# First-layer attention products four heads side by side, row sums from a tile of ones and from GpSimd, and the low parts of the second layer's queries and keys subtracted by GpSimd

## Chip, core and metric

The kernel runs on one core of one Trainium2 chip. The metric is the device time of one execution in microseconds; three executions of the kernel before gave 1474.76, 1475.09 and 1475.23 us, median 1475.09 us. The core's engines are TensorE (PE, with its weight loads shown apart as PEld), VectorE (DVE), ScalarE (ACT), GpSimd (POOL) and SyncE (SP, which here only issues DMAs).

## The reference

Two transformer layers over a sequence of 2048 tokens of width 128, all in float32. Each line of the sketch ends in a layer norm over the residual sum.

```python
x = layernorm(x + attention0(x))   # 8 heads in 2 groups, keys and values from 32 latents per group, causal softmax
x = layernorm(x + ffn0(x))         # 128 -> 352 -> 128, silu(gate) * up, inputs and weights rounded to blockwise FP4
x = layernorm(x + attention1(x))   # 16 heads of 8 in 4 groups, biases, softmax over all 2048 keys
x = layernorm(x + experts(x))      # 8 experts 128x128, softmax gate with a threshold of 0.1
```

In both attentions `scores = q k^T * scale`, `probs = softmax(scores)`, `y = probs v`. The kernel keeps `exp(scores - max)` and divides by its row sum (the denominator) at the end.

## The kernel before

**Tiling.** Queries are worked in chunks `c` of QC = 512 (NC = 4 chunks), keys in tiles `kt` of P = 128 (16 tiles). Heads come in groups `g` of HG = 4. One *iteration* is one `(layer, c, g)`. The first layer has 8 iterations and is causal: chunk `c` sees `4 (c + 1)` key tiles, of which the last four are *diagonal* (narrower: 512, 384, 256, 128 queries, and their triangle is zeroed by `clip` on POOL). The second layer has 16 iterations of 16 key tiles.

**One unit** is a key tile of one head. It is a score product on PE (L726 in the first layer, `KO0` by `QO`; L730 in the second, `KO1` by `Q1`; float32r) into a score bank of PSUM, an exponential on ACT (L926) into one of the 8 slots of `PR`, and a product with the values on PE (L749). The first layer has 2 score banks, the second 3. The product with the values is full float32, so each is two matmul instructions in a trace. A score product of unit `u` waits for the exponential of unit `u - 2` (first layer). An exponential waits until the product of the unit 8 earlier has read its slot.

**Values and denominators.** `V0[:, tile, g, :]` is VW0 = 64 wide: 32 latents and then ones, so that column 32 of the result is the denominator. Two heads stand side by side on the columns of PE (64 each), and two banks (`OUT_BANKS` 4 and 5) hold the four heads. In the second layer the values are VW1 = 32 wide (8 values, then ones), and four heads stand side by side in one bank.

**Order.** One list of steps is made at build time and each engine walks through it in order. `iteration` yields the four scores of a tile, with *side steps* spread between them, and behind every `SIDE_BY_SIDE[layer]` scores (2 in the first layer, 4 in the second) the products of as many heads of the tile before. Side steps use 4 further PSUM banks in turn (`side_full`, `side_free`). Most of them are `max`: the next iteration's scores laid out queries by keys (PE L655 in the first layer, L650 in the second), whose row maxima DVE takes (L1161, on the diagonal L1158). The others are the projections (`q0`, `k0`, `v0`, `q1`, `k1`, `v1`), the output of the iteration before (`out_copy` by ACT into `OS`, transposes L661, `out0` or `out1` on DVE), and the rest of the layer for the chunk before (`attended0`: output projection, norm, quantisation of x, gate and up; `rest0`: quantisation of h, down, norm, `k1`, `v1`; `chunk1`: the second layer's norm, gate and experts).

**High and low parts.** A float32 query or key is kept as a float32r number and a remainder. For `k0` and `q0` only rows of the result are subtracted. For `q1` and `k1` (32 and 16 of them, 128x512 each) ACT writes rows into `Q1` or `KO1` with a mask as the scale (L840, L848), and DVE then writes bank plus bias minus that into the same tile (L1102, `tails`) and frees the side bank.

**POOL** has `clip` (L996, 128 in the first layer), `rstd` (L988, 16) and the sums over experts (L1003, L1005).

## Time and profile before

| | |
|---|---|
| median of the three timed runs | 1475.09 us |
| the profiled execution's own time | 1470.66 us |
| its span, first to last instruction | 1468.9 us |
| PE busy | 1311.4 us, 89% |
| DVE busy | 1088.7 us, 74% |
| ACT busy | 845.8 us, 58% |
| POOL busy | 110.8 us, 8% |
| mean granted TensorE clock | 0.929 of full speed |

The page divides the span among engines, follows back the chain of work that ended last, and groups instructions by line and shape. The idle time shown beside an instruction is that of its engine just before it, with what released it. A matmul's own duration contains its pipeline; how often matmuls follow each other is read from their starts.

### The profile page before, as it was taken

The numbers are of one execution on the slowest core, as the hardware profiler recorded it, in microseconds if no ns is written. First come the engines' busy times: TensorE is split into PE (matmuls) and PEld (weight loads), VectorE is DVE, ScalarE is ACT, GpSimd is POOL, SyncE is SP. The second block draws the span as 40 slices with busy tenths as digits, with TensorE's granted clock in tenths as the row PEclk, the third lists the DMA queues.
The fourth block names the chain that finished last, engine by engine and source line by source line (L and its number), as shares of the span: only waits on it lengthen the run. The fifth ranks groups of instructions, "written<-read, shape, count | busy, mean of one in ns | idle before, by whom it ended". The sixth has DMA issues, their size and how long they took to land.

```text
span 1468.9 us, 19049 instructions
## 1 busy us (share of the span) xinstructions
PE 1311.4 (89%) x6337; PEld 563.3 (38%) x6337; DVE 1088.7 (74%) x2289; ACT 845.8 (58%) x1621; POOL 110.8 (8%) x227
## 2 busy tenths in 40 slices
PE   4688889889999965899999999999999999999884
PEld 3354445344443432433333333333433333333322
DVE  3677696688645668778888788888879888987324
ACT  2445535554555421177777666777666776777660
POOL 2010010001010100000000002000110000000033
PEclk9669899899999975689999999999999999999897
DMA  3000000000000000000000000000000000000000
GB/s 100 1 1 1 1 1 1 0 1 1 1 1 1 0 1 0 1 1 1 2 1 1 1 1 9 1 1 1 1 1 8 1 1 2 1 1 1 1 8 8
DMA packets 9010, 6.13 MB, mean 4 GB/s; under 512 B 2184, under 2 KB 8272, under 8 KB 8912
## 3 DMA queue, kind: packets, MB, share of 16 engines
q1 hardware_dynamic: 8912, 4.91, 1.2%
q8 instruction: 51, 0.84, 0.2%
q14 instruction: 47, 0.39, 0.1%
HBM read 3.66 MB, written 1.05 MB: 3 GB/s over the span
## 4 chain that ended last, share of the span: by engine, by line
PE 71%; DVE 15%; ACT 7%; issue 4%; POOL 1%; DMA 1%; SPq 1%; DVEq 0%; POOLq 0%; ACTq 0%
PE ps L749 24%; PE ps L730 16%; PE ps L650 8%; DVE MP L1161 7%; PE ps L726 6%; ACT PR L926 4%; PE ps L655 4%; PE ps L646 2%; PE ps L712 2%; ACT QO L825 1%; PE ps L661 1%; PE ps L679 1%; DVE ps L1158 1%; PE ps L615 1%; PE ps L690 1%
## 5 line engine op out<-in xcount | busy, mean ns | idle before, releaser
L926 ACT ACTIVATE PR<-ps 128x512 f32<-128x512 f32 (+2 forms) x1344 | 699.1, 585 | 414.1 <-PE ps L730 224.3
L1161 DVE TENSOR_REDUCE MP<-ps 128x1 f32<-128x512 f32 x1216 | 764.2, 682 | 133.9 <-PE ps L650 87.4
L749 PE MATMUL ps<-PR,V 128*32 128x512 f32 (+2 forms) x2688 | 435.6, 605 | 0.7 <-ACT OS L825 0.7
L730 PE MATMUL ps<-Q,KO 64*128 64x512 f32 x1024 | 363.1, 466 | 26.6 <-ACT PR L926 20.6
L650 PE MATMUL ps<-KO,Q 64*128 64x512 f32 x1024 | 354.5, 447 | 16.3 <-DVE MP L1161 12.2
L730 PEld LDWEIGHTS ps<-Q,KO 64*128 64x128 f32 x1024 | 153.6, 186 | 350.3 <-ACT PR L926 290.3
L650 PEld LDWEIGHTS ps<-KO,Q 64*128 64x128 f32 x1024 | 164.4, 191 | 85.0 <-DVE MP L1161 47.9
L726 PE MATMUL ps<-QO,KO 97*128 97x512 f32 (+3 forms) x320 | 144.7, 464 | 21.2 <-ACT PR L926 18.8
L655 PE MATMUL ps<-KO,QO 96*128 96x512 f32 (+2 forms) x320 | 127.9, 441 | 19.5 <-DVE QO L1137 13.7
L749 PEld LDWEIGHTS ps<-PR,V 128*32 128x32 f32 (+1 forms) x2688 | 74.1, 116 | 130.6 <-issue 60.4
L726 PEld LDWEIGHTS ps<-QO,KO 97*128 97x128 f32 x320 | 62.8, 201 | 152.0 <-ACT PR L926 97.0
L655 PEld LDWEIGHTS ps<-KO,QO 96*128 96x128 f32 x320 | 66.7, 214 | 43.2 <-DVE QO L1137 15.3
L1158 DVE CUSTOM_DVE_ANT_0 ps<-ps,mask_qk 128x128 f32<-128x128 f32 (+3 forms) x128 | 62.8, 493 | 20.8 <-PE ps L655 20.4
L996 POOL TENSOR_SCALAR_AFFINE_SELECT PR<-PR 128x128 f32<-128x128 f32 x128 | 39.0, 307 | 396.2 <-ACT PR L926 395.3
L988 POOL TENSOR_TENSOR RS<-VE,const 128x4 f32<-128x4 f32 x16 | 16.2, 1010 | 660.0 <-DVE VE L1091 660.0
L1102 DVE SCALAR_TENSOR_TENSOR Q<-ps,bq,Q 128x512 fp32r<-128x512 f32 x32 | 24.0, 750 | 39.9 <-ACT Q L840 30.2
L1137 DVE TENSOR_TENSOR QO<-ps,QO 32x512 fp32r<-32x512 f32 x32 | 22.0, 688 | 25.7 <-ACT QO L825 25.4
L1003 POOL TENSOR_TENSOR qa<-qa 128x512 f32<-128x512 f32 (+2 forms) x24 | 19.7, 821 | 225.3 <-DVE XQ L1206 216.2
L712 PE MATMUL ps<-ew,XQT 128*128 128x512 f32 x64 | 36.2, 665 | 0.0
L646 PE MATMUL ps<-XT,WQ 128*128 128x512 f32 x64 | 35.6, 638 | 0.0
L825 ACT ACTIVATE HQT<-ps 128x256 f32<-128x256 f32 (+2 forms) x36 | 11.0, 354 | 37.4 <-PE ps L685 33.8
L840 ACT ACTIVATE Q<-ps,bq_low,const 128x512 fp32r<-128x512 f32 x32 | 24.9, 777 | 7.7 <-PE ps L646 7.7
(179 smaller groups left out, 748.7 us busy)
## 6 DMA issues: line engine op xcount, KB each, us to landing
Q<-MR SPq DMA_DIRECT2D x64, 2.0 KB
result<-V SPq DMA_DIRECT2D x4, 256.0 KB, 2.3
H<-in_L_attn_wq SPq DMA_DIRECT2D x1, 512.0 KB, 6.7
HQT<-in_L_attn_wo SPq DMA_DIRECT2D x1, 512.0 KB, 5.0
ew<-in_L_ffn_expert_w SPq DMA_DIRECT2D x1, 512.0 KB
bq<-in_L_attn_bq SPq DMA_DIRECT2D x12, 0.1 KB
wd<-in_L_ffn_w_down SPq DMA_DIRECT2D x1, 176.0 KB, 3.7
wg<-in_L_ffn_w_gate SPq DMA_DIRECT2D x1, 128.0 KB, 4.4
```

Of the source, the lines that this page charges most:

```text
L646: last = nc.tensor.matmul(bank[:, :], WQ13[:, g, pair, :, :], XT[:, c * QC:(c + 1) * QC], start=True, stop=True)
L650: last = nc.tensor.matmul(bank[:, :], Q1[rows, buf, h // 2, q * P:(q + 1) * P], KO1[rows, g, kc * QC:(kc + 1) * QC], start=True, stop=True)
L655: last = nc.tensor.matmul(bank[:, 0:n], QO[0:SHIFT, buf, h, q * P:(q + 1) * P], KO0[0:SHIFT, g, kc * QC:kc * QC + n], start=True, stop=True)
L712: last = nc.tensor.matmul(bank[:, :], X2T[:, q * P:(q + 1) * P], ew[:, 4 * e:4 * e + 4, :], start=True, stop=True)
L726: m = nc.tensor.matmul(dst[:, q0:QC], KO0[:, g, kt * P:(kt + 1) * P], QO[:, buffer_of(0, it), h, q0:QC], start=True, stop=True)
L730: m = nc.tensor.matmul(dst[:, :], KO1[rows, g, kt * P:(kt + 1) * P], Q1[rows, it, h // 2, :], start=True, stop=True)
L749: nc.tensor.matmul(dst, VO[layer][:, kt, g, :], PR[:, u % NP_RING, q0:QC], start=kt == 0, stop=kt == key_tiles(layer, c) - 1).then_inc(pv_ ...
L825: return nc.scalar.activation(out, in_, ACT.Copy)
L926: nc.scalar.activation(PR[:, u % NP_RING, q0:QC], ps[:, 8 - nb + u % nb, q0:QC], ACT.Exp, scale=SCALE[layer]).then_inc(exp_done, 1)
L996: nc.gpsimd.affine_select(block, block, [[1, P]], ALU.is_ge, nothing, base=0, channel_multiplier=-1).then_inc(clipped, 1)
L1158: v.tensor_tensor_reduce(bank[:, 0:w], bank[:, 0:w], mask_qk[:, QC - w:QC], 1.0, LOWEST, ALU.add, ALU.max, MP[:, buf, h, q, kc:kc + 1]).th ...
L1161: v.tensor_reduce(MP[:, buf, h, q, kc:kc + 1], bank[:, 0:w], AX, ALU.max).then_inc(free, 1)
```

## The change

1. In the first layer the values are 32 wide (`VW0` 64 to 32, no ones in `V0`), four heads stand side by side, and their products go into one bank (5) once per tile. `SIDE_BY_SIDE` becomes (4, 4).
2. The first layer's denominators come from products of a tile of ones (`ones`, 128x32) with the same `PR` slots, four heads side by side into bank 4 (`denominators`).
3. For some tiles (`by_pool`: below the diagonal, tile 0 and the odd ones) there is no such product. POOL adds the `PR` slots of these tiles up (`add_up`, into `ADDED[h]`: two halves of `ew` and two of a new tile `more`), and at the iteration's end one product of ones with each sum adds them in. Chunks 1, 2 and 3 have 3, 5 and 7 such tiles in each of their two iterations, and 8, 16 and 24 additions of 128x512. An exponential waits as well until POOL has read its slot (`added`).
4. For `q1` and `k1` ACT writes two tiles from the bank (`WHOLE`, a ring of two, with the bias; then `Q1` or `KO1` as before) and frees the bank; POOL subtracts one from the other. PE's `max` waits for POOL (`tailed`) in place of DVE.
5. `out0` becomes one reciprocal over the bank of denominators and one multiplication over that of products, in place of two of each.
6. The experts' weights are loaded when the second layer's products begin, since `ew` serves as `ADDED` before. Some weights move into other tiles' space.

```diff
-VW0, VW1 = 64, 32
+VW0, VW1 = 32, 32
+        WHOLE = (sb("WHOLE", [P, QC])[:, :], flat(wgu[:, 0:QC // D, :]))
+        more = sb("more", [P, NE, D])
+        ADDED = [x[:, j * QT:(j + 1) * QT, :].rearrange("p e d -> p (e d)") for x in (ew, more) for j in range(2)]
+        def by_pool(layer, c, kt):
+            return layer == 0 and kt < c * QT and (kt == 0 or kt % 2 == 1)
...
+            def denominators(c, kt, n, u, q0):
+                last = kt == key_tiles(0, c) - 1
+                if not by_pool(0, c, kt):
+                    if diagonal(0, c, kt):
+                        pe.wait_ge(clipped, n.clips + clips_at[0] + HG - 1)
+                    else:
+                        pe.wait_ge(exp_done, n.units + u + 4 + HG)
+                    for h in range(HG):
+                        nc.tensor.matmul(ps[h * VW0:(h + 1) * VW0, OUT_BANKS[0], q0:QC], ones[:, :], PR[:, (u + h) % NP_RING, q0:QC],
+                                         start=kt == (2 if c else 0), stop=last and c == 0)
+                if last and c > 0:
+                    added_at[0] += added_in(c)
+                    pe.wait_ge(added, n.added + added_at[0])
+                    for h in range(HG):
+                        nc.tensor.matmul(ps[h * VW0:(h + 1) * VW0, OUT_BANKS[0], :], ones[:, :], ADDED[h],
+                                         start=False, stop=True)
...
-                if layer == 0:
-                    dst = ps[(h % 2) * VW0:(h % 2 + 1) * VW0, OUT_BANKS[h // 2], q0:QC]
-                else:
-                    dst = ps[h * VW1:(h + 1) * VW1, OUT_BANKS[0], q0:QC]
+                if layer == 0 and h == 0:
+                    denominators(c, kt, n, u, q0)
+                dst = ps[h * VW1:(h + 1) * VW1, OUT_BANKS[1 - layer], q0:QC]
...
+                if kind in BY_POOL:
+                    t = tails_at[0]
+                    if t >= len(WHOLE):
+                        act.wait_ge(tailed, t + 1 - len(WHOLE))
+                    dst, bias, low_bias, low = of_parts(item)
+                    nc.scalar.activation(WHOLE[t % len(WHOLE)], bank, ACT.Identity, bias=bias)
+                    i = nc.scalar.activation(dst, bank, ACT.Identity, bias=low_bias, scale=low)
+                    tails_at[0] += 1
...
                         act.wait_ge(pv_done, n.units + u + 1)
+                        if u >= NP_RING and add_of[u - NP_RING]:
+                            act.wait_ge(added, add_of[u - NP_RING])
...
+            def add_up(h, unit, sums, first):
+                p = PR[:, unit % NP_RING, :]
+                pool.wait_ge(exp_done, unit + 5)
+                if first:
+                    nc.gpsimd.tensor_tensor(ADDED[h], PR[:, (unit - HG) % NP_RING, :], p, ALU.add).then_inc(added, 1)
+                else:
+                    pool.wait_ge(added, sums + 1 - HG)
+                    nc.gpsimd.tensor_tensor(ADDED[h], ADDED[h], p, ALU.add).then_inc(added, 1)
...
+                        if by_pool(layer, c, kt):
+                            if kt == 1 and h == 0:
+                                pool.wait_ge(pv_done, NP_RING + n.units + units - HG)
+                            if kt > 0:
+                                add_up(h, n.units + units, n.added + sums, kt == 1)
+                                sums += 1
...
+                    if kind in BY_POOL:
+                        pool.wait_ge(side_free[k % NS], n.side // NS + k // NS + 2)
+                        dst = of_parts(step)[0]
+                        nc.gpsimd.tensor_tensor(dst, WHOLE[tails % len(WHOLE)], dst.bitcast(f32),
+                                                ALU.subtract).then_inc(tailed, 1)
...
-            def tails(dst, bank, bias):
-                return v.scalar_tensor_tensor(dst, bank, bias, dst.bitcast(f32), ALU.add, ALU.subtract)
...
                 if kind == "out0":
-                    b = item[1]
-                    o = bank.rearrange("p (q h l) -> p q h l", q=QT, h=2)
-                    rec = OR[:, :, 0:2]
-                    link(v.reciprocal(rec, o[:, :, :, LAT]))
-                    v.tensor_tensor(ON[:, :, :].rearrange("p q (h l) -> p q h l", l=LAT)[:, :, 2 * b:2 * b + 2, :],
-                                    o[:, :, :, 0:LAT], rec.unsqueeze(3).broadcast_to([P, QT, 2, LAT]), ALU.mult).then_inc(free, 1)
+                    o = bank.rearrange("p (q h l) -> p q h l", q=QT, h=HG)
+                    if item[1] == 0:
+                        v.reciprocal(OR[:, :, :], o[:, :, :, 0]).then_inc(free, 1)
+                        return
+                    v.tensor_tensor(ON[:, :, :].rearrange("p q (h l) -> p q h l", l=LAT), o,
+                                    OR[:, :, :].unsqueeze(3).broadcast_to([P, QT, HG, LAT]), ALU.mult).then_inc(free, 1)
```

PE in the last iteration of the first layer (c = 3, g = 1), before: one key tile, two heads at a time behind every second score (L726 is a score, L650 a `max` of the second layer, L749 a product).

```order
L749 MATMUL ps<-PR,V 64x512 x2
L726 MATMUL ps<-QO,KO 128x512
L650 MATMUL ps<-KO,Q 128x512
L726 MATMUL ps<-QO,KO 128x512
L749 MATMUL ps<-PR,V 64x512 x2
```

The same place after the change (L762 is the score, L686 the `max`, L721 transposes of H, L778 the product with ones, L802 the product with the values): two key tiles, the first with products alone behind it, the second with denominators too.

```order
L802 MATMUL ps<-PR,V 32x512 x4
L762 MATMUL ps<-QO,KO 128x512
L686 MATMUL ps<-KO,Q 128x512
L762 MATMUL ps<-QO,KO 128x512 x2
L686 MATMUL ps<-KO,Q 128x512
L762 MATMUL ps<-QO,KO 128x512
L721 MATMUL ps<-const,H 128x128 x2
L721 MATMUL ps<-const,H 96x128
L778 MATMUL ps<-PR,ones 32x512 x4
L802 MATMUL ps<-PR,V 32x512 x4
```

Between two bursts of products there are now four scores, where there were two; a `max` stands behind two of the four.

POOL from c = 2, g = 0 to the start of c = 3, g = 0, before (L996 is `clip`, L988 is `rstd`):

```order
L996 AFFINE_SELECT PR<-PR 128x128 x24
L988 TENSOR_TENSOR RS<-VE,const 128x4
L996 AFFINE_SELECT PR<-PR 128x128 x8
L988 TENSOR_TENSOR RS<-VE,const 128x4
```

After the change, from the end of c = 2, g = 1 into the first seven key tiles of c = 3, g = 0 (L1081 is `clip`, L1063 `rstd`, L1118 the subtraction for `k1`, L1070 and L1073 the additions):

```order
L1081 AFFINE_SELECT PR<-PR 128x128
L1118 TENSOR_TENSOR KO<-wgu,KO 128x512
L1070 TENSOR_TENSOR ew<-PR 128x512 x2
L1070 TENSOR_TENSOR more<-PR 128x512 x2
L1073 TENSOR_TENSOR ew<-ew,PR 128x512
L1063 TENSOR_TENSOR RS<-VE,const 128x4
L1073 TENSOR_TENSOR ew<-ew,PR 128x512
L1073 TENSOR_TENSOR more<-more,PR 128x512 x2
```

POOL's queue, which held short clips and the `rstd`, now has four additions for every second key tile, and the `rstd` stands among them.

## Rows read from the trace of the kernel before

**Rows 1.** The page's fourth part: the chain that ended last, by engine.

```profile
PE 71%; DVE 15%; ACT 7%; issue 4%; POOL 1%; DMA 1%; SPq 1%; DVEq 0%; POOLq 0%; ACTq 0%
```

**Rows 2.** Busy time by stage: start:end, length, engines' busy us (count), PE clock.

```profile
118.00:173.00 55.00, 46.31 (x198) 23.85 (x197) 40.52 (x106) 33.84 (x60) 5.91 (x17) 0.95 0.00 1
173.00:233.00 60.00, 52.39 (x220) 27.92 (x220) 49.07 (x134) 23.21 (x51) 6.06 (x17) 0.90 0.00 1
233.00:307.00 74.00, 66.20 (x264) 31.34 (x262) 49.60 (x123) 42.85 (x75) 5.87 (x17) 0.93 0.00 1
307.00:374.00 67.00, 64.38 (x278) 32.05 (x277) 58.90 (x151) 32.01 (x67) 6.33 (x17) 0.97 0.00 1
374.00:448.00 74.00, 70.14 (x284) 30.97 (x284) 38.91 (x96) 41.28 (x78) 5.66 (x17) 0.98 0.00 1
448.00:523.00 75.00, 73.97 (x287) 29.69 (x287) 44.02 (x98) 38.57 (x77) 5.63 (x17) 1.00 0.00 1
523.00:626.00 103.00, 67.45 (x179) 33.74 (x181) 77.23 (x175) 15.30 (x27) 2.01 (x2) 0.63 0.00 0
626.00:1371.00 745.00, 719.69 (x4030) 278.75 (x4030) 633.06 (x1106) 533.40 (x1025) 28.44 (x37) 0.99 0.01 2
```

**Rows 3.** Instructions grouped by line and shape: count, busy us, mean ns, idle before.

```profile
L749 PE MATMUL ps<-PR,V 128*32 128x512 f32 x2048 | 276.7, 613 | 0.0
L749 PE MATMUL ps<-PR,V 128*64 128x512 f32 x448 | 126.5, 644 | 0.7 <-ACT OS L825 0.7
...
L840 ACT ACTIVATE Q<-ps,bq_low,const 128x512 fp32r<-128x512 f32 x32 | 24.9, 777 | 7.7 <-PE ps L646 7.7
L1102 DVE SCALAR_TENSOR_TENSOR Q<-ps,bq,Q 128x512 fp32r<-128x512 f32 x32 | 24.0, 750 | 39.9 <-ACT Q L840 30.2 <-PE ps L650 8.9 <-PE ps L664 0.8
...
L825 ACT ACTIVATE OS<-ps 128x512 f32<-128x512 f32 x32 | 18.4, 608 | 7.3 <-PE ps L749 7.2
...
L1003 POOL TENSOR_TENSOR qa<-qa 128x512 f32<-128x512 f32 x8 | 10.2, 1273 | 224.1 <-DVE XQ L1206 216.2 <-DVE qa L1212 7.8
```

**Rows 4.** Timeline in c = 3, g = 0: start us, duration us, instruction.

```profile
405.23 0.72 PE L726 MATMUL ps<-QO,KO 97*128 97x512 f32 x2
...
405.79 0.39 PE L655 MATMUL ps<-KO,QO 96*128 96x512 f32 x1
...
406.11 1.08 PE L749 MATMUL ps<-PR,V 128*64 128x512 f32 x4
...
407.12 0.73 PE L726 MATMUL ps<-QO,KO 97*128 97x512 f32 x2
```

**Rows 5.** Timeline in c = 3, g = 1.

```profile
465.18 0.50 PE L726 MATMUL ps<-QO,KO 97*128 97x512 f32 x1
...
465.61 0.50 PE L650 MATMUL ps<-KO,Q 64*128 64x512 f32 x1
465.72 0.60 ACT L926 ACTIVATE PR<-ps 128x512 f32<-128x512 f32 x1 [0.84 <-PE ps L726]
...
466.04 0.50 PE L726 MATMUL ps<-QO,KO 97*128 97x512 f32 x1
...
466.47 1.08 PE L749 MATMUL ps<-PR,V 128*64 128x512 f32 x4
```

**Rows 6.** Timeline in the second layer, products four side by side.

```profile
689.39 1.07 PE L749 MATMUL ps<-PR,V 128*32 128x512 f32 x8
...
690.39 0.50 PE L730 MATMUL ps<-Q,KO 64*128 64x512 f32 x2
...
690.92 2.06 ACT L926 ACTIVATE PR<-ps 128x512 f32<-128x512 f32 x4 [0.76 <-PE ps L730]
...
691.57 0.18 PEld L730 LDWEIGHTS ps<-Q,KO 64*128 64x128 f32 x1 [0.43 <-ACT PR L926]
```

**Rows 7.** All clips on POOL: durations in ns (minimum/median/maximum), first and last start.

```profile
L996 POOL TENSOR_SCALAR_AFFINE_SELECT PR<-PR x128: 292/292/673, 53.1 to 521.0; 128x128 f32<-128x128 f32 x128
```

**Rows 8.** Timeline of POOL and DVE where a clip met a quantising step.

```profile
205.37 0.49 POOL L996 TENSOR_SCALAR_AFFINE_SELECT PR<-PR 128x128 f32<-128x128 f32 x1 [4.61 <-ACT PR L926]
...
205.38 0.34 DVE L1069 TENSOR_SCALAR qc<-qc 128x352 f32<-128x352 f32 x1
```

More of the change, by code:

```diff
@@ L475, in __init__ @@
                 self.heads = sum(k in IN_PARTS for k in kinds)
+                self.tails = sum(k in BY_POOL for k in kinds)
                 self.rstd = sum(k in ("y0", "down", "y1", "stats") for k in kinds)
@@ L478, in __init__ @@
                 self.logits = kinds.count("logits")
+                self.added = sum(s[0] == "scores" and s[5] > 0 and by_pool(s[1], s[2], s[5]) for s in steps)
                 self.clips = sum(s[0] == "scores" and diagonal(s[1], s[2], s[5]) for s in steps)
@@ L507, in build @@
         program = padded(program)
+        UNITS0 = sum(s[:2] == ("scores", 0) for s in program)
         def parts(engine, walk):
@@ L551, in walk @@
             def walk(steps, n, lag):
-                k, chunks = 0, 0
+                k, chunks, units, experts = 0, 0, 0, False
                 for step in steps:
+                    units += step[0] == "scores"
+                    if step[0] == "products" and step[1] == 1 and not experts:
+                        experts = True
+                        sp.wait_ge(pv_done, NP_RING + UNITS0)
+                        sp.dma_start(ew[:, :, :], A["L1_ffn_expert_w"].rearrange("e k n -> k e n")).then_inc(ld["experts"], 16)
                     if step[0] == "shift":
@@ L808, in walk @@
                         pe.wait_ge(ld["attn1"], N_ATTN1)
-                        pe.wait_ge(ld["moe"], 64)
+                        pe.wait_ge(ld["moe"], 48)
+                    if step == ("expert", 0, 0):
+                        pe.wait_ge(ld["experts"], 16)
                     if kind == "wgT":
@@ L1008, in walk @@
             def walk(steps, n, lag):
-                k, rs, tiles, units = 0, 0, 0, 0
+                k, rs, tiles, tails, units, sums = 0, 0, 0, 0, 0, 0
                 for step in steps:
@@ L1012, in walk @@
                     if kind == "scores":
-                        if diagonal(*step[1:3], step[5]):
-                            clip(n.units + units, first_query(*step[1:3], step[5]))
+                        _, layer, c, g, it, kt, h = step
+                        if diagonal(layer, c, kt):
+                            clip(n.units + units, first_query(layer, c, kt))
+                        if by_pool(layer, c, kt):
+                            if kt == 1 and h == 0:
[3 more added lines that the diff above has]
+                                sums += 1
                         units += 1
```

81 lines of the change are left out of this document (47 added, 34 removed).

## The prediction

> **What bounds the kernel now.** I read the chain that ended last first: 71% of it is PE and 15% DVE [rows 1], so PE time is what counts, if it is saved where PE is the one that is late. That is read by stage [rows 2]. The six rows from 118 to 523 us are the iterations c = 1 to 3 of the first layer, two per chunk. In c = 3 PE is busy 70.1 of 74 us and 74.0 of 75, and DVE only 38.9 and 44.0: whatever PE saves there comes off the time. In the g = 1 iterations of c = 1 and c = 2 DVE is busy 49.1 of 60 us and 58.9 of 67, because they carry the quantisation of h and more maxima than scores. There a PE that is faster soon meets DVE. From 523 to 626 us, the end of the first layer, DVE leads (77 of 103 us, PE clock 0.63). From 626 to 1371 us, the second layer, PE is busy 720 of 745 us, DVE 633 and ACT 533. The change alters no PE work there.
>
> **Products of the first layer.** A pair of 64-wide products over 512 queries starts at 406.11 and the next score at 407.12 us: 1.01 us [rows 4]. Four 32-wide ones start at 689.39, the next score at 690.39: 1.00 us [rows 6]. The busy times agree: 126.5 us over 448/4 = 112 pairs is 1.13, 276.7 over 2048/8 = 256 fours is 1.08 [rows 3], each with some 0.1 us of the last one's pipeline in it. So a tile costs 2.02 us now, and will cost 1.00 if POOL sums it and 2.00 if the tile of ones does. The chunks 1 to 3 have 2 x (3 + 5 + 7) = 30 summed tiles. That is 30 x 1.02 = 30.6 us less PE time, against 6 x 1.00 = 6 us for the last products with the sums. The 26 other tiles of 512 queries and the narrow ones cost what they did. This 24.6 us is the gross term; the rest is about what becomes of it.
>
> **Bursts.** Two bursts per tile become one, with four scores between. That has two effects. From the first of two scores to the burst, with one maximum, takes 406.11 - 405.23 = 0.88 us for three matmuls, so the steps beside a burst are some 0.1 us longer than those within; one burst fewer saves about 0.1 to 0.2 us a tile. Against it, with two score banks the third score must wait for the first one's exponential, which used to run under the pair between. The score starts at 465.18, its exponential at 465.72 (0.54 later) and takes 0.60 [rows 5]; another waiting score starts (691.57) 0.05 after the exponential that it needs ends (690.92 + 0.60). So the third score starts no earlier than 0.54 + 0.60 + 0.05 = 1.19 us after the first. The fourth waits for an exponential that ends 0.52 later (four take 2.06 [rows 6]), so 1.71, and the burst starts 0.32 after it (405.79 to 406.11 [rows 4]): 2.03 us.
>
> - c = 3, g = 0: a tile has four scores and mostly two maxima. Now it takes 2 x 1.89 = 3.78 us [rows 4]. Afterwards 2.03 + 1.00 = 3.03 (summed, -0.75) or 4.03 (+0.25). With 7 summed, 6 others and the last product: -5.3 + 1.5 + 1.0 = -2.8 us.
> - c = 3, g = 1: matmuls of different row counts follow each other in 0.43 us (465.18, 465.61, 466.04), so half a tile takes 1.29 + 1.01 = 2.30 us and a tile 4.60. Afterwards, as the order shows, a maximum stands behind two of the four scores: 1.19 + 3 x 0.43 = 2.48, and 3.48 (-1.12) or 4.48 (-0.12). -7.8 - 0.7 + 1.0 = -7.5 us.
> - c = 2 and c = 1, g = 0: about one maximum or more behind each score, so that PE reaches the third score at 1.0 us or later anyway and the exponential is covered. I take -1.12 and -0.12: -5.6 - 0.5 + 1.0 = -5.1 us, and -3.4 - 0.2 + 1.0 = -2.6 us.
> - c = 2 and c = 1, g = 1: the same on PE, but DVE has 8.1 and 10.9 us of idle time [rows 2] in many short pieces, and gives back 4 x 0.75 = 3 us in each for the keys' subtractions. I take 2 us and 1 us.
>
> The sum is -2.8 - 7.5 - 5.1 - 2.6 - 2 - 1 = -21.0 us. The chunk c = 0 has no summed tile and is counted as nothing: its PE time is the same, and the waits for the clips of all four heads lie one tile behind.
>
> **The additions on POOL.** The nearest row is the experts' sum, 128x512 with two inputs in SBUF: 1.27 us [rows 3]. Four of them take 5.1 us per two tiles, and two tiles will take 3.03 + 4.03 = 7.1 us, so POOL keeps up in the steady part. At an iteration's start it does not quite: tile 0's slots are freed only by the additions of tile 1, so the exponential of head 3 of tile 2 waits for the fourth addition. That ends 4 x 1.27 = 5.1 us after tile 1's first exponential, where ACT would like the slot about 4 us after it. The output steps of the iteration before stretch these tiles; I take 0.4 us each in six iterations, +2.4 us (bounds 0 and 1.1 each, 6.6 in all). The clips and `rstd` queue behind additions. The first diagonal tile's clips come some 5 us after the last additions begin, and its products a tile later: nothing. `rstd` also holds up the additions behind it until DVE's statistics are there; a slot is wanted back two tiles (7 us) later, which covers it.
>
> **POOL against DVE.** A clip takes 292 ns at the median but 0.49 us where it met a VectorE step from SBUF to SBUF (205.37 us) [rows 7, 8]. The additions are four times longer, and DVE's quantising steps may stand behind them: in c = 1 and 2, g = 1 DVE is the one that can least afford it. The values of 1 and 2 us above already hold some of this. The Trainium skill, in "SBUF — State Buffer", section "Who interferes with whom", says more: a DVE step with two SBUF inputs or in a 2-port mode and a GpSimd step share a port pair, and whoever comes second is blocked for the whole of the other. By the clip's row the trace agrees as far as it goes; by the rule, 16 additions of 1.27 us in 67 us would meet a third of some 24 such steps and hold each for about 0.6 us, 5 us of DVE in c = 2, g = 1, and that iteration would then gain nothing.
>
> **The low parts.** Per tile DVE loses 0.75 us, ACT gains a copy between the 0.61 us of an output copy and the 0.78 of the masked one, POOL gains 1.27 [rows 3]. For 24 to 28 queries in the second layer: ACT has 745 - 533 = 212 us of idle time there and takes 28 x 0.65 = 18 more. PE's third score bank and the burst of products (1.00 us) cover most of it. DVE, 85% busy, loses 21 us. Both can hold PE; I take -1 us, bounds -8 (half of DVE's relief reaches PE) and +9 (half of ACT's copies do). The queries are asked for half an iteration ahead, so POOL's latency is hidden. At the first layer's end it is not: the last keys are needed at once, and ACT's copy and POOL's 1.27 in place of DVE's 0.75 make them 0.6 + 1.27 - 0.75 = 1.1 us later, of which DVE's own relief gives back half: +0.5 us. `out0` costs DVE what it did within 0.3 us and is off the path. The experts' load moves to 626 us, some 200 us before its first use, and waits for products long done.
>
> **Sum.** -21.0 + 2.4 - 1 + 0.5 = -19.1 us. Against the profiled execution's own 1470.66 us (span 1468.9, 1.8 around it) that is 1451.6. The runs' median, 1475.09, is 4.4 higher, and I forecast for such runs: 1475.1 - 19.1 = 1456 us.
>
> **Rivals.**
> - *The gross term arrives.* The exponentials' wait is hidden by the maxima and DVE does not limit: 24.6 us, and one burst fewer in some 80 tiles at 0.1 to 0.15, so -33 us, 1442 us. For it: PE above 95% in c = 2, g = 1 and c = 3. Against: 1.19 us is longer than the 0.9 us that PE needs for two scores and two maxima.
> - *Only c = 3 gains.* DVE, slowed by the additions, or the PE clock (0.90 to 0.95 in c = 1 and the start of c = 2) eats the rest: -10 us with the start's waits, 1466 us. For it: DVE at 82 and 88% in rows 2, and the clip's 0.49 us.
> - *POOL becomes the bound (slower).* Place: the `PR` slots of odd tiles. Two tiles take 7.1 us, so it decides once four additions take longer, at 1.77 us each; there are 24 such pairs. At 2.0 us it costs 24 x 0.9 = 22 us and the change is about even; at 2.2 us 24 x 1.7 = 41, and 1475 - 19 + 41 = 1497 us. For it: the clip's maximum of 673 ns is over twice its median. Against: 1.27 us in every row of the experts' sums.
> - *Nothing in net*: the second layer's +9 and the bound of the start's waits, 1475 - 21 + 6.6 + 9 + 1 = 1471 us or more.
>
> **Chances and range.** Forecast (1448 to 1461) 0.45, the gross term (1438 to 1448) 0.17, only c = 3 (1461 to 1470) 0.23, nothing in net (1470 to 1478) 0.07, POOL the bound 0.08. The range 1441 to 1470 leaves out the last two and a little of the second. A measurement here can tell about 0.2%, 3 us. Faster than that: 0.45 + 0.17 + 0.23 + 0.02 = 0.87; within it 0.05; slower 0.08.
>
> **What would show it.** The groups of the changed profile: 32-wide products 1.00 us apart in the first layer, additions at 1.27 us. Stages: c = 3, g = 1 some 7 us shorter and g = 0 only some 3, with PE idle before scores on ACT there; c = 1 and c = 2, g = 1 nearly as long as before; the second layer within 2 us of 745. Wrong if ACT waits for POOL's additions beyond each iteration's third tile, if the additions take 1.8 us or more, or if DVE's quantising steps are much longer than they are (0.34 us in rows 8).

## The result: 1.06% slower, and the profile after

The changed kernel takes 1490.89 us (median of 4 runs, 1490.33 to 1490.99) against 1475.16 for the kernel before, a ratio of 1.0106 with a 95% interval of 1.0089 to 1.0124. The forecast was 1456 us, faster. The profiled execution took 1490.83 us. Now and then an execution runs at a low clock throughout (e2's profiled one took 1605.3 us at 0.72); medians and ratios here leave these out. The page's first and fourth part of the changed kernel:

```profile
PE 1299.7 (87%) x6785; PEld 564.5 (38%) x6785; DVE 1090.1 (73%) x2225; ACT 870.2 (58%) x1669; POOL 294.6 (20%) x371
...
PE 67%; DVE 17%; ACT 8%; issue 4%; POOL 2%; DMA 1%; SPq 1%; DVEq 0%; POOLq 0%; ACTq 0%
```

PE is busy 11.7 us less than before, and the kernel is 20 us longer in these two profiles (the kernel before's profiled execution is 4.5 us under its median). PE's share of the last chain fell from 71% to 67% [rows 1] and DVE's rose from 15% to 17%.

**Where.** I cut both traces at the copies of the results to `OS`, which end each iteration. Windows of the changed kernel (start:end, length, busy us of PE, PEld, DVE, ACT, POOL with counts, PE clock): c = 0, g = 1; then c = 1, 2, 3 with g = 0 and 1 each; then all seven.

```profile
89.70:120.00 30.30, 27.17 (x142) 16.38 (x142) 22.43 (x66) 11.53 (x38) 3.93 (x13) 0.76 0.00 1
120.00:176.30 56.30, 45.13 (x247) 23.87 (x247) 41.55 (x102) 33.51 (x59) 16.15 (x25) 0.91 0.00 1
176.30:240.50 64.20, 50.70 (x266) 28.71 (x266) 50.97 (x127) 25.83 (x55) 22.25 (x29) 0.87 0.00 1
240.50:315.10 74.60, 63.24 (x329) 31.66 (x328) 55.59 (x120) 42.53 (x74) 26.76 (x33) 0.91 0.00 1
315.10:393.10 78.00, 68.26 (x340) 34.88 (x341) 60.35 (x143) 34.19 (x70) 31.49 (x37) 0.85 0.00 1
393.10:463.70 70.60, 63.90 (x367) 30.12 (x367) 46.04 (x98) 42.87 (x81) 38.39 (x43) 0.98 0.00 1
463.70:537.60 73.90, 69.87 (x368) 29.40 (x367) 49.33 (x87) 40.17 (x82) 42.13 (x46) 0.98 0.00 1
89.70:537.60 447.90, 388.28 (x2054) 195.01 (x2053) 326.26 (x741) 230.62 (x453) 181.10 (x225) 0.90 0.00 1
```

The same cut of the kernel before, all seven (c = 2, g = 1 stands in [rows 2], within 0.1 us).

```profile
89.30:522.50 433.20, 399.58 (x1638) 191.76 (x1637) 303.52 (x767) 223.71 (x438) 39.26 (x116) 0.95 0.00 1
```

The lengths, c = 0, g = 1 to c = 3, g = 1: before 28.0, 54.6, 60.3, 73.9, 66.9, 74.7, 74.8; after 30.3, 56.3, 64.2, 74.6, 78.0, 70.6, 73.9. So the first layer lost 14.7 us, 11.1 of them in c = 2, g = 1. PE is busy 11.3 us less in it and idle 26.0 more (447.9 - 388.3 = 59.6, against 33.6), and its clock is 0.90 in place of 0.95. At two levels, 1.2 and 2.4 GHz, a mean of 0.90 means that the lower one held for about 447.9 x 0.10 x 2 = 90 us; before it was about 433.2 x 0.05 x 2 = 43 us. In c = 2, g = 1 alone PE is idle 9.7 us (78.0 - 68.3), before 2.7, and busy 4 us longer on 4 us less work. From the first layer's last copy to the start of the second layer's last iteration it is 856.6 us, before 856.7; the last iteration takes 55.9 in place of 49.9. It has the same instructions; 20 us around its start ran at 0.51 of the clock where those of before had 0.74 (first row after, second row before):

```profile
1391.00:1411.00 20.00, 19.34 (x69) 7.36 (x73) 2.58 (x13) 11.11 (x23) 0.00 (x0) 0.51 0.00 0
```

```profile
1374.00:1394.00 20.00, 18.19 (x80) 6.73 (x80) 2.58 (x13) 12.46 (x25) 0.00 (x0) 0.74 0.01 1
```

**How.** The timeline of the changed kernel in c = 2, g = 1 (start us, us, instruction, in brackets the engine's idle time before it and what ended it):

```profile
327.26 0.51 DVE L1172 TENSOR_TENSOR qa<-qa,qc 128x352 f32<-128x352 f32 x1
...
327.88 2.78 POOL L1073 TENSOR_TENSOR ew<-ew,PR 128x512 f32<-128x512 f32 x2 [4.85 <-ACT PR L1001]
...
328.31 1.23 DVE L1174 TENSOR_TENSOR qa<-qa,qc 128x352 f32<-128x352 f32 x1
...
329.57 1.47 DVE L1176 TENSOR_TENSOR H<-qa,qs 128x352 f32<-128x352 f32 x1
330.62 2.78 POOL L1073 TENSOR_TENSOR more<-more,PR 128x512 f32<-128x512 f32 x2
...
331.72 0.55 PE L721 MATMUL ps<-const,H 128*128 128x128 f32 x3 [2.88 <-DVEq L1181]
...
332.26 1.12 PE L778 MATMUL ps<-PR,ones 128*32 128x512 f32 x8
...
333.14 1.95 PE L802 MATMUL ps<-PR,V 128*32 128x512 f32 x8
```

The same kind of step takes 0.51 us before POOL's additions begin, and 1.23 and 1.47 us under them. PE needs the quantised `H` for a transposition that stands in its queue ahead of the rest, and waits 2.88 us. Behind it the four products take 1.95 us where they took 1.07 [rows 6]: the granted clock is 1.00 from 326 to 333 us and 0.57 from 333 to 337. Wait and lower clock come together here. What waited, and for what (changed kernel, first layer; engine, line, released by: us in total, times, longest):

```profile
PE ps L762 <- ACT PR L1001: 24.9, 22, 4.1
PE ps L721 <- DVEq L1181: 12.7, 6, 4.0
PE ps L691 <- DVE MP L1252: 4.8, 9, 0.9
```

and of the kernel before:

```profile
PE ps L726 <- ACT PR L926: 18.8, 7, 3.7
PE ps L685 <- DVEq L1081: 3.5, 4, 1.6
...
PE ps L655 <- DVE MP L1161: 0.9, 3, 0.5
```

H's transpositions wait 9 us more, the scores 6 (e4 has these without any sum), the maxima 4. PE never waits for an addition, and ACT does so once, for 0.2 us. Groups of DVE steps by shape, changed kernel (count | busy, mean ns), and behind them those of the kernel before:

```profile
L1176 DVE TENSOR_TENSOR H<-qa,qs 128x352 f32<-128x352 f32 x12 | 9.3, 775 | 0.1
L1174 DVE TENSOR_TENSOR qa<-qa,qc 128x352 f32<-128x352 f32 x13 | 8.9, 684 | 0.2
...
L1169 DVE TENSOR_SCALAR qc<-qc 128x352 f32<-128x352 f32 x13 | 7.6, 586 | 0.2
```

```profile
L1074 DVE TENSOR_TENSOR qa<-qa,qc 128x352 f32<-128x352 f32 x13 | 6.8, 519 | 0.2
...
L1076 DVE TENSOR_TENSOR H<-qa,qs 128x352 f32<-128x352 f32 x12 | 6.2, 518 | 0.1
L1069 DVE TENSOR_SCALAR qc<-qc 128x352 f32<-128x352 f32 x13 | 4.4, 337 | 0.2
```

### The profile page after: what moved, and what is told of

It reads as the page before. It is cut to its first block, busy times and chain, and to the rows that moved or that the text cites. A ratio compares the mean times of both kernels' runs of the same rounds, so it can differ in the third digit from the quotient of the medians.

```text
span 1489.1 us, 20173 instructions
## 1 busy us (share of the span) xinstructions
PE 1299.7 (87%) x6785; PEld 564.5 (38%) x6785; DVE 1090.1 (73%) x2225; ACT 870.2 (58%) x1669; POOL 294.6 (20%) x371
## 3 DMA queue, kind: packets, MB, share of 16 engines
HBM read 3.66 MB, written 1.05 MB: 3 GB/s over the span
## 4 chain that ended last, share of the span: by engine, by line
PE 67%; DVE 17%; ACT 8%; issue 4%; POOL 2%; DMA 1%; SPq 1%; DVEq 0%; POOLq 0%; ACTq 0%
PE ps L802 20%; PE ps L766 16%; PE ps L686 7%; DVE MP L1252 7%; ACT PR L1001 5%; PE ps L762 4%; PE ps L691 3%; PE ps L778 2%; PE ps L748 2%; PE ps L682 2%; DVE ps L1249 1%; PE ps L697 1%; ACT QO L889 1%; PE ps L715 1%; PE ps L726 1%
## 5 line engine op out<-in xcount | busy, mean ns | idle before, releaser
L766 PE MATMUL ps<-Q,KO 64*128 64x512 f32 x1024 | 367.2, 471 | 27.2 <-ACT PR L1001 21.0
L686 PE MATMUL ps<-KO,Q 64*128 64x512 f32 x1024 | 351.5, 445 | 18.3 <-DVE MP L1252 13.5
L802 PE MATMUL ps<-PR,V 128*32 128x512 f32 (+1 forms) x2688 | 365.1, 616 | 0.0
L686 PEld LDWEIGHTS ps<-KO,Q 64*128 64x128 f32 x1024 | 163.5, 191 | 77.8 <-DVE MP L1252 40.6
L762 PE MATMUL ps<-QO,KO 97*128 97x512 f32 (+3 forms) x320 | 147.1, 469 | 27.5 <-ACT PR L1001 24.9
L691 PE MATMUL ps<-KO,QO 96*128 96x512 f32 (+2 forms) x320 | 131.3, 449 | 27.4 <-DVE QO L1233 14.7
L762 PEld LDWEIGHTS ps<-QO,KO 97*128 97x128 f32 x320 | 64.3, 203 | 129.0 <-ACT PR L1001 68.0
L1118 POOL TENSOR_TENSOR Q<-WHOLE,Q 128x512 fp32r<-128x512 f32 x16 | 20.5, 1280 | 452.0 <-ACT Q L923 452.0
L802 PEld LDWEIGHTS ps<-PR,V 128*32 128x32 f32 x2688 | 60.2, 111 | 120.6 <-issue 65.9
L1081 POOL TENSOR_SCALAR_AFFINE_SELECT PR<-PR 128x128 f32<-128x128 f32 x128 | 38.9, 309 | 181.9 <-ACT PR L1001 181.0
L1073 POOL TENSOR_TENSOR ew<-ew,PR 128x512 f32<-128x512 f32 x36 | 47.2, 1331 | 73.0 <-ACT PR L1001 73.0
L778 PE MATMUL ps<-PR,ones 128*32 128x512 f32 (+3 forms) x400 | 49.6, 571 | 1.2 <-POOL PR L1081 1.2
L1073 POOL TENSOR_TENSOR more<-more,PR 128x512 f32<-128x512 f32 x36 | 48.0, 1351 | 0.3 <-ACT PR L1001 0.3
L1118 POOL TENSOR_TENSOR Q<-wgu,Q 128x512 fp32r<-128x512 f32 x16 | 20.6, 1290 | 133.3 <-ACT Q L923 133.3
L1063 POOL TENSOR_TENSOR RS<-VE,const 128x4 f32<-128x4 f32 x16 | 16.2, 1015 | 121.8 <-DVE VE L1191 121.8
```

The lines of the kernel that those rows point to most:

```text
L686: last = nc.tensor.matmul(bank[:, :], Q1[rows, buf, h // 2, q * P:(q + 1) * P], KO1[rows, g, kc * QC:(kc + 1) * QC], start=True, stop=True)
L691: last = nc.tensor.matmul(bank[:, 0:n], QO[0:SHIFT, buf, h, q * P:(q + 1) * P], KO0[0:SHIFT, g, kc * QC:kc * QC + n], start=True, stop=True)
L762: m = nc.tensor.matmul(dst[:, q0:QC], KO0[:, g, kt * P:(kt + 1) * P], QO[:, buffer_of(0, it), h, q0:QC], start=True, stop=True)
L766: m = nc.tensor.matmul(dst[:, :], KO1[rows, g, kt * P:(kt + 1) * P], Q1[rows, it, h // 2, :], start=True, stop=True)
L778: nc.tensor.matmul(ps[h * VW0:(h + 1) * VW0, OUT_BANKS[0], q0:QC], ones[:, :], PR[:, (u + h) % NP_RING, q0:QC], start=kt == (2 if c else 0 ...
L802: nc.tensor.matmul(dst, VO[layer][:, kt, g, :], PR[:, u % NP_RING, q0:QC], start=kt == 0, stop=kt == key_tiles(layer, c) - 1).then_inc(pv_ ...
```

## The experiments

Each was timed with the kernel before on the same chip; ratios to it are what I compare (0.1% is 1.5 us; the runs lie on several chips). "The split kernel" is e6.

| kernel | bursts a tile | sums on POOL | low parts | median us | ratio (95%) |
|---|---|---|---|---|---|
| after | 1 | c = 1, 2, 3 | POOL | 1490.9 | 1.0106 (1.0089 to 1.0124) |
| e2 | 1 | c = 1, 2, 3 | DVE | 1488.1 | 1.0098 (1.0074 to 1.0122) |
| e1 | 1 | none | POOL | 1484.2 | 1.0074 (1.0046 to 1.0102) |
| e4 | 1 | none | DVE | 1481.6 | 1.0050 (1.0035 to 1.0065) |
| e3 | 1 | fills for additions | DVE | 1466.5 | 0.9962 (0.9942 to 0.9981) |
| e5 | 1 | c = 3 | DVE | 1467.8 | 0.9969 (0.9952 to 0.9986) |
| e9 | 2 | c = 1, 2, 3 | DVE | 1478.4 | 1.0026 (1.0009 to 1.0044) |
| e6 | 2 | none | DVE | 1467.4 | 0.9969 (0.9950 to 0.9988) |
| e8 | 2 | c = 3; c = 2, g = 0 | DVE | 1465.8 | 0.9954 (0.9934 to 0.9974) |
| e7 | 2 | c = 3 | DVE | 1460.9 | 0.9925 (0.9898 to 0.9951) |
| e16 | as e7 | | | 1461.6 | 0.9921 (0.9901 to 0.9942) |
| e10 | 2 | c = 3 | POOL | 1468.2 | 0.9956 (0.9937 to 0.9974) |
| e11 | 2 | c = 3, 8 of 12 tiles | DVE | 1469.3 | 0.9974 (0.9955 to 0.9993) |
| e12 | 2 | 48 idle, c = 1, 2 | DVE | 1483.5 | 1.0064 (1.0044 to 1.0084) |
| e13 | 2 | none, e12's start | DVE | 1468.2 | 0.9960 (0.9941 to 0.9979) |
| e14 | 2 | 48 idle fills, c = 1, 2 | DVE | 1479.7 | 1.0040 (1.0019 to 1.0062) |
| e15 | 2 | 48 idle, c = 3 | DVE | 1467.6 | 0.9960 (0.9939 to 0.9980) |

### e1, e2, e4: the parts of the change, one by one

e1 takes no sums (first pair of lines, in `by_pool`); e2 gives the low parts back to DVE, whose step is again as before; e4 does both.

```diff
-            return layer == 0 and kt < c * QT and (kt == 0 or kt % 2 == 1)
+            return layer == 0 and False and kt < c * QT and (kt == 0 or kt % 2 == 1)
...
-        IN_PARTS = ("q0", "k0")
-        BY_POOL = ("q1", "k1")
+        IN_PARTS = ("q0", "k0", "k1", "q1")
+        BY_POOL = ()
```

> No tile is summed on POOL: the product of ones is made for all 16 tiles, and the six last products with the sums fall away. POOL keeps the low parts. Theory A (POOL's additions hold up VectorE's quantising steps, PE then waits for H and its clock falls): c = 2, g = 1 comes back from 78 us to 68 to 72, c = 1, g = 1 from 64 to about 61, while c = 3 gets 4 to 5 us longer per iteration; in all 1476 to 1486 us. Rival B (the single burst per tile and the waits for exponentials cost the time): the time rises by the 24 us of PE products, to 1505 or more. Rival C (the low parts on ACT and POOL cost it): also above 1490.

> The changed kernel with the low parts of queries and keys as before the change (one copy by ACT, the subtraction by VectorE); the sums stay on POOL. Theory A: little changes, 1486 to 1493 us, c = 2, g = 1 still above 75 us. Rival C (the low parts cost it): 1475 to 1480 us.

> Both undone: products of ones for all tiles, low parts by VectorE; what is left of the change is four heads side by side, one burst per tile and the denominators in their own bank. PE does the same amount of products as the kernel before. Theory A: 1472 to 1480 us. Rival B (the burst): 1485 to 1492 us, with PE idle before scores on the exponentials.

Without any sum the kernel is still slower than before by 0.5 to 0.7%, though PE's work is the same. That points at the one long burst, which e6 tests; e4 lies above the theory's range and below the rival's. e2's ratio differs from that of the change by 0.0008, e1's from e4's by 0.0024: 1 and 3.5 us for the low parts, both within the noise. e1 over the seven iterations, in which its c = 2, g = 1 takes 68.8 us:

```profile
93.60:536.50 442.90, 397.58 (x2246) 196.11 (x2245) 290.65 (x741) 230.09 (x453) 56.12 (x129) 0.93 0.00 1
```

DVE is busy 290.7 us without the sums and 326.3 with them.

### e3: the additions as fills

e2, with every addition replaced by a fill of about the same length (1408 numbers, 1.27 us; the additions take 1.28 to 1.35) that reads nothing; each fill also waits for the one before, and the denominators are not computed.

```diff
-                    nc.gpsimd.tensor_tensor(ADDED[h], ADDED[h], p, ALU.add).then_inc(added, 1)
+                    nc.gpsimd.memset(more[:, :, :], 1.0).then_inc(added, 1)
```

> Low parts by VectorE, and each addition on POOL replaced by a fill of 1408 numbers per partition that reads nothing (1.27 us by the fills at the start of the kernel before: 951 ns for 1024 and 1804 for 2048 numbers), so the denominators are not the reference's; all waits are kept. Theory A in its strict form (VectorE steps with two inputs in SBUF are blocked only by a POOL step that reads SBUF): they run at 0.52 us again, only the steps from one SBUF tile to another are still late, and the time is 1465 to 1476 us. Rival D (the waits between PE, ACT and POOL for the slots cost the time, whatever POOL does in its 1.27 us): within 4 us of the run with the real additions.

The same waits of PE and ACT and nearly the same time on POOL, but no reads of SBUF: 0.9962 against 1.0098, 20 us. So these waits are not what costs, and the larger part of the price hangs on what POOL reads. Fills are not free either: PE has 24.6 us less to do than in e4, and 13 us arrive, so I estimate that the 96 fills cost some 12 us. The seven iterations of e3, and DVE's groups in them:

```profile
89.60:525.00 435.40, 386.91 (x2054) 194.19 (x2053) 318.15 (x756) 223.31 (x438) 160.54 (x212) 0.90 0.00 1
```

```profile
L1174 DVE TENSOR_SCALAR qc<-qc 128x352 f32<-128x352 f32 x13 | 7.7, 596 | 0.2
L1179 DVE TENSOR_TENSOR qa<-qa,qc 128x352 f32<-128x352 f32 x13 | 6.8, 521 | 0.2
```

Under fills the steps with two inputs are as fast as before (521 ns against 519) while those with one input are as slow as under additions (596, 586, before 337). DVE is busy 16.8 us longer than in e4 (301.4 us).

### e6: two bursts per tile again

e4, with the product of ones behind the second score and the four products behind the fourth.

```diff
-        SIDE_BY_SIDE = (P // VW0, P // VW1)
+        SIDE_BY_SIDE = (2, P // VW1)
...
+                if layer == 0 and h != 2:
+                    return
+                for j in (range(HG) if layer == 0 else [h]):
...
+                    nc.tensor.matmul(dst, VO[layer][:, kt, g, :], PR[:, (u + j - h) % NP_RING, q0:QC],
```

> The kernel with tiles of ones everywhere and no work on GpSimd beyond before's (1481.6 us), with its one burst of eight products per key tile cut into two of four again: the denominators' product stands behind the second score's place of the tile, the four heads' products behind the fourth. PE work is the same as before the change and as in the kernel with one burst. Theory (the third score waits for the first one's exponential behind one long burst, some 7 us in all): 1472 to 1477 us, c = 3, g = 1 back from 77.8 to about 75 us. Rival (the 7 us come from where the denominators' products wait for all four exponentials, or from the clock, and not from the number of bursts): 1480 to 1484 us.

0.9969 against e4's 1.0050: the long burst costs 12 us, more than the 5 to 10 expected, and with two bursts the tiles of ones are even 0.3% below before (I have no shown cause for that). The windows over the seven iterations, e4, then e6:

```profile
91.20:529.90 438.70, 396.30 (x2246) 195.83 (x2245) 301.36 (x755) 222.67 (x439) 38.75 (x115) 0.93 0.00 1
```

```profile
90.80:517.10 426.30, 391.59 (x2246) 183.77 (x2245) 301.40 (x754) 223.33 (x439) 38.82 (x115) 0.96 0.00 1
```

The same 2246 matmuls: PE is idle 42.4 us against 34.7, and busy 4.7 us longer at a lower clock. The scores wait 21 times for an exponential in e4 (25.4 us in all), 7 times in e6 (18.9):

```profile
PE ps L762 <- ACT PR L1004: 25.4, 21, 4.0
```

```profile
PE ps L762 <- ACT PR L1009: 18.9, 7, 3.8
```

### e5, e7, e8, e9, e16: where the sums pay

The condition of `by_pool` becomes `c == 3` (e5 with one burst; e7 and e16 with two), `c == 3 or c == 2 and g == 0` (e8) and `c > 0` (e9).

> One burst per tile as in the change, sums in c = 3 alone, low parts on DVE. Theory with both causes: 1481.6 less 7 to 10 us in c = 3: 1471 to 1475 us, about 7 above the split one. If bursts cost nothing: as the split one. If additions cost as much in c = 3 as elsewhere: 1482 us or more.

> The split kernel with GpSimd's sums in chunk c = 3 alone (14 summed tiles, 48 additions), where DVE is busy only 44 of 75 us, and the low parts on DVE. Theory (the additions hurt where DVE is nearly the bound, c = 1 and 2, and hurt little in c = 3): 14 x 1.0 - 2 x 1.0 = 12 us less PE in c = 3, of which some 8 to 10 arrive: 1464 to 1468 us, below before. Rival (additions that read SBUF cost their gain wherever they run): 1472 us or more.

> As the split kernel with sums in c = 3, and sums also in c = 2, g = 0, where DVE was busy 49.6 of 74 us before. Theory: 5 - 1 = 4 us less PE there, arriving in half: 1462 to 1467 us. Rival (wherever quantising steps run, an addition delays them and with them PE): 1468 us or more, above the kernel with c = 3 alone.

> The split kernel with the sums in all of chunks 1 to 3, so the change with its bursts cut in two and the low parts on DVE. It has 16 summed tiles more than the one with sums in c = 3 alone, 16 - 4 = 12 us less PE work. Theory: these sums cost more than they bring, 1470 to 1478 us, against 1460.9 with sums in c = 3 alone, and some 13 us below the change. Rival (the long burst made the additions hurt): 1455 us or less.

> The kernel with two bursts per tile, sums in c = 3 alone and low parts on DVE, once more, unchanged. Theory: 1458 to 1464 us, a ratio of 0.992 to 0.995. Rival (its first measurement was a lucky one): above 1467 us.

e7 and e5 came out some 3 us below what was expected of them, e8 and e16 within it, and e9 at the upper edge. With sums in c = 3 alone the kernel is faster than before, 0.9925 and again 0.9921: this is the version that beats both. Against e6 that is 6.5 us; with one burst (e5 against e4) even 12. The sums of c = 1 and 2 turn it round: e9 against e7 is +0.0101, 15 us, although PE has 12 us less to do, so I estimate the price of these 48 additions at 27 us. e8 is 1.0029 times e7, with intervals that overlap: in c = 2, g = 0, where DVE is busy two thirds of the time, a sum brings nothing that shows. The windows over the seven iterations, e7, then e9:

```profile
89.20:507.60 418.40, 380.76 (x2150) 182.13 (x2148) 318.77 (x755) 223.17 (x438) 101.00 (x163) 0.96 0.00 1
```

```profile
88.60:529.70 441.10, 390.22 (x2054) 189.90 (x2053) 336.91 (x755) 224.06 (x439) 163.64 (x211) 0.91 0.00 1
```

e9 has 96 matmuls fewer and PE is busy 9.5 us longer, at a clock of 0.91, and idle 13.2 us longer. What grew among its waits ends at DVE: waits for the quantised `H` and x grow by 8.1 us (9.5 and 2.5 against 3.9 and none) and those for maxima by 3.4, while waits for exponentials shrink by 1.2, ACT waits for an addition for 0.2 us at most and PE never. DVE is busy 18.1 us longer.

### e10, e11: two variants of the best

e10 is e7 with the low parts as in the change; e11 sums tiles 0, 1, 3, 4, 6, 7, 9 and 10 (`kt % 3 != 2`).

> Two bursts per tile and sums in c = 3, as in the kernel of 1460.9 us, but the low parts with ACT and GpSimd as in the change. Theory (nearly neutral, as between the change and the same with the low parts on DVE): 1459 to 1464 us. Rival (ACT's 44 copies and GpSimd's subtractions cost 3 us or more): 1465 us or above.

> As the kernel with two bursts and sums in c = 3, with tiles 0, 1, 3, 4, 6, 7, 9, 10 summed in place of 0 and the odd ones: 8 of 12 in place of 7, and two summed tiles in a row, so eight additions (10.2 us) in three tiles of some 4 to 4.6 us. Theory: 2 x 1.0 us less PE, 56 additions, a little back to longer DVE steps: 1459 to 1461 us, no difference that can be measured. Rival (the slots of two summed tiles in a row come free too late): 1463 us or more, with ACT waiting for the additions.

e10: +0.0031 against e7, 4.6 us, where the theory said neutral; the intervals overlap, but three pairs (+0.0008, +0.0024, +0.0031) point the same way. e11: +0.0049, 7 us, against my expectation. In the profiles its c = 3, g = 0 takes 76.6 us in place of e7's 69.6 at a clock of 0.93 in place of 0.98, and DVE is busy 5.4 us longer there. ACT waits for the additions no longer than in e7 (0.2 us), so it is not the rival's late slots. That execution took 1463.5 us, 6 us under e11's median, so the first cause stays open.

### e12 to e15: additions that nobody waits for

The split kernel with 48 additions of a constant tile, where the change has its additions of c = 1 and 2. Their result isn't used.

```diff
+                        if idle_add(layer, c, kt):
+                            pool.wait_ge(exp_done, n.units + units + 5)
+                            pool.wait_ge(added, n.added + sums + 1)
+                            nc.gpsimd.tensor_tensor(ADDED[3], ADDED[2], ADDED[2], ALU.add).then_inc(added, 1)
```

e13 has none left but the same start; e14 has fills in their place; e15 has the additions in c = 3. The idle additions read one tile twice and turned out shorter than the real ones, and shorter than the fills that stand for them (e12, then e14):

```profile
L1124 POOL TENSOR_TENSOR more<-more 128x512 f32<-128x512 f32 x48 | 50.7, 1055 | 95.6 <-ACT PR L1013 92.1
```

```profile
L1124 POOL MEMSET more<- 128x1408 f32 x48 | 61.1, 1274 | 89.3 <-ACT PR L1013 86.2
```

> The split kernel with tiles of ones everywhere (1467.4 us), its PE work untouched, and 48 additions of 128x512 on GpSimd in chunks 1 and 2, at the tiles where the change has them, that read a constant tile and whose result nobody reads or waits for. They start as the exponentials come, like the real ones. Theory (additions that read SBUF block DVE's two-input and tensor-scalar steps, PE then waits for H and the maxima, and its clock falls): 8 to 15 us slower than the split kernel, 1476 to 1482 us, though nothing waits for the additions. Rival (the sums cost through waits for slots, for the sums and for the last products): within 2 us of 1467 us.

> The kernel with idle additions, with none left (its start with the one fill of the constant tile stays). Theory (the additions themselves cost the 14 us): as the split kernel, 1464 to 1471 us. Rival (the start's fill, or chance, shifts PE's clock for the rest): 1476 us or more.

> The kernel with idle additions in chunks 1 and 2, each replaced by a fill of the same length (1408 numbers, 1.27 us) that reads nothing. Theory (two-input DVE steps contend only with a GpSimd step that reads; the tensor-scalar ones with both): the two-input steps stay at 519 ns, and about a third to a half of the additions' cost is left: 1470 to 1477 us. Rival (any GpSimd work of that length costs the same): 1480 to 1484 us.

> The split kernel with 48 idle additions in chunk 3 in place of chunks 1 and 2. DVE is busy 39 and 44 of 74 us there. Theory (DVE has the time, so PE does not wait and its clock stays): within 3 us of the split kernel, 1464 to 1471 us, though DVE's steps are as much longer. Rival (additions cost the same wherever they run): 1476 us or more.

e12 costs 0.0104 over its control, 15 us, though PE, ACT and DVE wait for none of the additions (the clips and `rstd` queue behind them on POOL, but PE's weight loads wait 6.4 us for clips in e12 and in e15 alike, 5.0 in e13, and nobody waits for `rstd`). The same 48 additions in c = 3 cost nothing that shows (0.9960 and 0.9960). Windows of the seven iterations: e13, e12, e15, e14.

```profile
89.10:515.40 426.30, 391.71 (x2246) 183.80 (x2245) 301.31 (x753) 223.47 (x438) 39.02 (x115) 0.96 0.00 1
```

```profile
88.60:532.70 444.10, 407.90 (x2246) 190.72 (x2245) 313.79 (x754) 224.22 (x439) 89.64 (x163) 0.92 0.00 1
```

```profile
88.90:523.00 434.10, 400.11 (x2246) 187.78 (x2245) 312.24 (x753) 223.80 (x438) 90.20 (x163) 0.94 0.00 1
```

```profile
89.30:529.50 440.20, 404.11 (x2246) 188.11 (x2245) 311.57 (x754) 223.96 (x439) 99.80 (x163) 0.93 0.00 1
```

DVE is busy 12.5 us more in e12 and 10.9 more in e15, so the blocking is nearly the same; only in c = 1 and 2 does it reach the time. And there it comes almost wholly as clock: PE is busy 16 us longer on the same matmuls (2.2 of them in c = 0, g = 1), and idle only 1.6 us longer (36.2 against 34.6; with the real additions, e9 against e7, it was 13.2). A caution: c = 0, g = 1 already differs between these four profiles (27.9, 30.3, 30.3, 28.6 us) where no addition runs, and e15's seven iterations are 8 us longer than e13's while the medians agree. How the clock falls in c = 0 differs from one execution to the next; only the medians say what an edit costs. In e12 and e15, which began alike, c = 1, g = 1 takes 67.5 and 60.6 us and c = 2, g = 1 takes 70.3 and 67.5.

e14 fell nearer the rival, just below its range: fills cost 0.0080 over the control, 12 us, additions 0.0104, 15 us. But a fill is a fifth longer than an idle addition, so this pair does not tell which share of the price the one-input steps have. That e2 and e3 lie 20 us apart and e12 and e14 only 3.5 goes with DVE's busy time: real additions hold it up by 35.5 us (e9 against e6, 301.4) and the same number of fills by 16.8 (e3 against e4); idle additions by 12.5 and their fills by 10.3 (e14 against e13). The fills cost about 12 us in both settings. The idle additions are a mild copy of the real ones: they give 15 of the estimated 27 us that the real ones cost in c = 1 and 2, and 12.5 of the 18.1 us that DVE loses there.

## Why the prediction was wrong

The kernels form a chain of single steps from before to after, in ratios: products as two bursts with tiles of ones (e6) -0.0031; sums in c = 3 (e7) -0.0044; sums in c = 1 and 2 (e9) +0.0101; one burst per tile (e2) +0.0072; low parts (after) +0.0008. Each step has some 0.0025 of uncertainty. The sum is +0.0106, in us -4.6 - 6.5 + 14.9 + 10.6 + 1.2 = 15.6. Another order of the steps gives other sizes: the burst costs 12 us without sums and 6.5 with those of c = 3 alone.

By iteration, from the lengths above: in c = 1 and 2 the forecast's terms were -2.6, -1, -5.1 and -2 us, the change +1.7, +3.9, +0.7 and +11.1; in c = 3 they were -2.8 and -7.5, the change -4.1 and -0.9; c = 0, g = 1, counted as nothing, took 2.3 us more. So 28 of the 36 us between forecast and result in the first layer lie in c = 1 and 2.

- **What bounds the kernel.** Right: PE in c = 3, DVE close to it in the g = 1 iterations of c = 1 and 2. That this bears on where a sum pays is what e7, e9 and e15 show.
- **The gross term.** Right in size. In the changed kernel it is 1.00 us at full clock from the burst's start to the next score (467.12 to 468.12), with the tile of ones 1.86 (491.16 to 493.02) where I had 2.00. In c = 3 the term was 14 x 1.02 - 2 = 12.3 us; PE's busy time fell by 10.8 (e7 against e6), and 6.5 us arrived.
- **Bursts.** The second step that failed: I made it -21 us net, with about nothing for the shape itself; one burst costs 12, 10.6 and 6.5 in three pairs (e4 and e6, e2 and e9, e5 and e7). The tile after the change was forecast well. In the changed kernel, c = 3, g = 1, it is 496.47 - 493.02 = 3.45 us (I had 3.48), with the third score 1.18 behind the first (1.19):

```profile
493.02 0.73 PE L762 MATMUL ps<-QO,KO 97*128 97x512 f32 x2
...
494.20 0.49 PE L762 MATMUL ps<-QO,KO 97*128 97x512 f32 x1 [0.45 <-ACT PR L1001]
494.63 0.50 PE L686 MATMUL ps<-KO,Q 64*128 64x512 f32 x1
495.05 0.49 PE L762 MATMUL ps<-QO,KO 97*128 97x512 f32 x1
495.48 1.07 PE L802 MATMUL ps<-PR,V 128*32 128x512 f32 x8
...
496.47 0.49 PE L762 MATMUL ps<-QO,KO 97*128 97x512 f32 x1
```

  It was the tile of before that was not: I doubled one half tile of 2.30 us [rows 5], and others take 2.10, since two scores in a row follow each other sooner than a score and a maximum:

```profile
458.78 0.73 PE L726 MATMUL ps<-QO,KO 97*128 97x512 f32 x2
459.44 0.50 PE L650 MATMUL ps<-KO,Q 64*128 64x512 f32 x1
459.87 1.08 PE L749 MATMUL ps<-PR,V 128*64 128x512 f32 x4
460.88 0.73 PE L726 MATMUL ps<-QO,KO 97*128 97x512 f32 x2
```

  Of the 12.4 us by which e4's seven iterations are longer than e6's, 3.3 are in c = 3, g = 1 and none in c = 3, g = 0. The rest is in c = 0 to 2; in all it is 7.7 us of idle PE, 6.5 of them waits for exponentials, and 4.7 us of lower clock. Part of it may be how these two executions began (30.4 and 27.9 us for c = 0, g = 1).
- **Additions on POOL.** On average 1.28 us each for the first and 1.33 to 1.35 for the running ones, 1.57 at most, so below the 1.77 of the slower rival. ACT waited 0.2 us for POOL, where I had counted 2.4: the lower bound.
- **POOL against DVE.** The step that failed first: what the additions do to DVE, and DVE to PE, in c = 1 and 2. I let it lie in "the values of 1 and 2 us above". DVE is busy 35.6 us more than in e1 over the seven iterations (326.3 against 290.7 us), 0.37 us for each of 96 additions. The Trainium skill's rule ("SBUF — State Buffer", section "Who interferes with whom") was weighed for one iteration, with 5 us of DVE in c = 2, g = 1, and the trace has 4.6 there (60.35 against 55.72 in e1), so the size was right. I stopped a step short twice. I did not apply it to c = 2, g = 0, where DVE lost 7.0 us and I took the full gain of 5.1, nor to c = 1. And I let the iteration "gain nothing", and left even that out of the sum, when DVE's loss came to PE as waits for `H` (three, 6.0 us in all; before 0.3) and as a lower clock, 0.85: 11.1 us lost. Lower clock had no term anywhere in the sum. The 24 steps that I counted in c = 2, g = 1 match its 16 two-input and 8 tensor-scalar ones of 128x352; the norm's tensor-scalar steps (128x128, 346 ns before and 524 after over the seven iterations) and the small ones on scales (128x22, one kind 178 and 430) I left out.
- **Low parts.** -0.5 us forecast, 1.2 to 4.6 measured in three pairs, within the bounds of -8 and +9. The second layer was neutral up to its last iteration, as forecast. That one took 55.9 us in the changed kernel and again in e10, but 47.9 in e1, which has the low parts on POOL too, and 47.6 to 50.0 in 14 others; it is the same instructions at another clock. Whether the low parts bring the long one about is not shown.
- **Rivals.** The slower case was built on POOL's own pace, which was never the bound. "Only c = 3 gains" named the right things, DVE slowed by additions and PE's clock, and stopped at the gain being eaten; nothing bounded it there. So the 0.08 for slower stood on a mechanism that did not act. The kernel with sums in c = 3 alone and two bursts took 1461 us, at the edge of that rival's 1461 to 1470: it is the rival's case, but another kernel.
